# Reordering the steps ahead of the first feed-forward jobs in a gated mLSTM + spiking feed-forward kernel

## The reference

```
x1 = x  + tanh(g_xattn) * mlstm(layernorm(x), ctx, ctx)
out = x1 + tanh(g_ffn)  * ffn(layernorm(x1))

mlstm(q, k, v), per sequence, 8 heads of 32:
  ig, fg = [q,k,v] @ igate_w.T + igate_b, [q,k,v] @ fgate_w.T + fgate_b
  cs     = cumsum(log_sigmoid(fg))
  log_D  = cs[t] - cs[s] + ig[s]   (s <= t, else -inf);  m = rowmax(log_D)
  C      = (q k^T / sqrt(32)) * exp(log_D - m)
  h      = C / (max(|rowsum(C)|, exp(-m)) + 1e-6) @ v
  return layernorm(h) * ln_scale

ffn(x): y = square(relu(x @ W_fc.T)) @ W_proj.T      (256 -> 1024 -> 256)
        5 leaky integrate-and-fire steps on y; returns spikes / 5
```

## Time and profile before

| | before |
|---|---|
| median of 3 runs | 660.52 us (660.26 to 661.48) |
| span of the profiled execution | 661.2 us |
| TensorE matmul busy | 589.5 us, 89% |
| VectorE busy | 542.4 us, 82% |
| GpSimd busy | 485.6 us, 73% |
| ScalarE busy | 484.4 us, 73% |
| mean granted TensorE clock | 0.972 |

### The profile page before, as it was taken

How to read it: one execution, slowest core, us unless ns; L and a number is a source line. 1 busy time by engine, 2 the same in 40 slices (tenths; PEclk the granted TensorE clock), 3 DMA queues, 4 the chain that set the end, 5 groups by cost and what they waited for, 6 DMA issues and landing times.

```text
span 661.2 us, 17665 instructions
## 1 busy us (share of the span) xinstructions
PE 589.5 (89%) x6032; PEld 483.9 (73%) x6032; DVE 542.4 (82%) x1222; ACT 484.4 (73%) x1011; POOL 485.6 (73%) x531
## 2 busy tenths in 40 slices
...
GB/s 262 225 52 115 97 115 70 176 83 96 83 156 169 74 91 147 208 26 139 115 186 60 96 110 155 159 86 80 150 207 18 97 101 148 63 2 33 1 33 32
DMA packets 73192, 71.33 MB, mean 108 GB/s; under 512 B 8720, under 2 KB 68752, under 8 KB 73104
## 3 DMA queue, kind: packets, MB, share of 16 engines
...
## 4 chain that ended last, share of the span: by engine, by line
PE 51%; DVE 10%; issue 10%; ACT 7%; POOL 7%; SPq 4%; DMA 2%; POOLq 0%; ACTq 0%; DVEq 0%
PE z_ps L997 16%; PE y_ps L1057 16%; PE arg_ps L702 3%; PE qk_ps L717 3%; POOL sq_lo L1040 3%; DVE spikes L1075 3%; PE misc_ps L463 2%; SPq L650 2%; PE misc_ps L529 2%; SPq L513 2%; ACT sq_hi L1019 1%; POOL c_lo L746 1%; PE pv_ps L766 1%; PE pv_ps L764 1%; PE pv_ps L841 1%
## 5 line engine op out<-in xcount | busy, mean ns | idle before, releaser
L1040 POOL TENSOR_TENSOR sq_lo<-w_raw,sq_hi 128x512 fp32r<-128x512 f32 (+1 forms) x96 | 113.0, 1178 | 66.2 <-ACT w_raw L1020 66.1
L746 POOL TENSOR_TENSOR c_lo<-decay 128x512 bf16<-128x512 f32 x128 | 132.5, 1042 | 22.4 <-DVE decay L736 22.2
L997 PE MATMUL z_ps<-x_hi,wfc_hi 128*128 128x512 f32 (+1 forms) x288 | 115.7, 402 | 5.9 <-ACT w_raw L1007 4.1
L1057 PE MATMUL y_ps<-sq_hi,wpr_hi 128*128 128x512 f32 (+1 forms) x288 | 115.1, 400 | 1.1 <-POOL sq_lo L1040 1.1
L997 PE MATMUL z_ps<-x_hi,wfc_lo 128*128 128x512 f32 (+1 forms) x288 | 107.2, 372 | 0.0
L997 PE MATMUL z_ps<-x_lo,wfc_hi 128*128 128x512 f32 (+1 forms) x288 | 107.2, 372 | 0.0
L1057 PE MATMUL y_ps<-sq_lo,wpr_hi 128*128 128x512 f32 (+1 forms) x288 | 106.8, 371 | 0.0
L1057 PE MATMUL y_ps<-sq_hi,wpr_lo 128*128 128x512 f32 (+1 forms) x288 | 106.6, 370 | 0.0
L736 DVE TENSOR_TENSOR decay<-qk_ps,decay 128x512 f32<-128x512 f32 x128 | 87.1, 680 | 18.5 <-PE qk_ps L717 14.4
L728 ACT ACTIVATE decay<-arg_ps,lqk_col 128x512 f32<-128x512 f32 x128 | 86.5, 676 | 19.7 <-PE arg_ps L705 19.1
L1040 POOL TENSOR_TENSOR sq_lo<-relu,sq_hi 128x512 fp32r<-128x512 f32 (+1 forms) x48 | 56.3, 1173 | 37.9 <-ACT relu L1020 35.2
...
## 6 DMA issues: line engine op xcount, KB each, us to landing
...
```

What stands on the lines that cost most here:

```text
L746: e.tensor_tensor(c_lo[i % NCH][:, :], c, top(c), ALU.subtract).then_inc(sem("c_lo"), 1)
L997: ins = e.matmul(z_ps[:, tokens(q)], lhsT, rhs, start=(n == 0), stop=(n == len(terms) - 1))
L1040: e.tensor_tensor(sq_lo[n % NSQ][:, tokens(q)], relu[n % NRE][:, tokens(q)], sq_hi[n % NSQ][:, tokens(q)].bitcast(fp32), ALU.subtract).the ...
L1057: ins = e.matmul(y[:, c, :], w[:, j, c * P:(c + 1) * P], h, start=(j == 0 and i == 0 and (c == 0 or whole)), stop=(j == FT - 1 and i == 2) ...
```

## The change

The first steps of all five lists are put into another order; the lists hold the same steps as before. The loop over `SLOTS` becomes a loop over 1 to 5, its borders are moved by one to three steps (the last steps of the head become the first of the loop body), and what its last passes did is written out behind it in the same order; `MISC_ORDER` is written in another way and gives the same order. From these entries on the order is the old one: SyncE `load_m_rows(4)`, ScalarE `relu_step(1, 2)`, VectorE `cmul(3, 3)`, TensorE `z_step(1, 3)`, GpSimd `state_lo(3)`. The diff of the heads, in the order SyncE, ScalarE, VectorE, TensorE, GpSimd:

```diff
         def sync_program(e):
   load_x(e, 0)
+  load_x(e, 1)
+  load_values(e, 0)
+  load_x(e, 2)
   load_k(e, 0)
-  load_x(e, 1)
-  load_x(e, 2)
   load_x(e, 3)
-  load_values(e, 0)
+  load_x(e, 4)
+  load_x(e, 5)
   load_values(e, 1)
   load_k(e, 1)
+  load_k(e, 2)
+  load_x(e, 6)
   setup_load_wfc(e)
-  load_k(e, 2)
-  load_x(e, 4)
-  load_x(e, 5)
+  load_k(e, 3)
   stack_heads(e, 0)
-  stack_heads(e, 1)
-  load_k(e, 3)
   setup_load_wproj(e)
   load_a_rows(e, 0)
-  load_x(e, 6)
+  stack_heads(e, 1)
   load_k(e, 4)
+  load_values(e, 2)
   load_k(e, 5)
-  load_values(e, 2)
   load_a_rows(e, 1)
+  stack_heads(e, 2)
+  load_m_rows(e, 2)
+  load_x(e, 7)
   load_values(e, 3)
-  stack_heads(e, 2)
+  load_a_rows(e, 2)
   load_k(e, 6)
-  load_m_rows(e, 2)
+  load_a_rows(e, 3)
+  load_values(e, 4)
   load_k(e, 7)
-  load_x(e, 7)
-  load_a_rows(e, 2)
+  load_m_rows(e, 3)
   stack_heads(e, 3)
-  load_a_rows(e, 3)
-  load_m_rows(e, 3)
+  load_k(e, 8)
   load_x(e, 8)
-  load_values(e, 4)
   stack_heads(e, 4)
   load_x(e, 9)
   load_values(e, 5)
-  load_k(e, 8)
   load_m_rows(e, 4)
   load_a_rows(e, 4)
   load_m_rows(e, 5)
...
   setup_tanh(e)
   ln1_rstd(e, 0)
   ln1_apply(e, 0)
+  ln1_apply(e, 1)
   q_hi(e, 0)
-  ln1_apply(e, 1)
   q_hi(e, 1)
   gates_out(e, 0)
   gates_out(e, 1)
-  split_wfc_hi(e, 0)
+  ln1_rstd(e, 1)
   gate_softplus(e, 0)
-  ln1_rstd(e, 1)
   am_split(e, 0, 0)
   ln1_apply(e, 2)
   am_split(e, 0, 2)
+  split_wpr_hi(e, 0)
   gate_softplus(e, 1)
+  load_m_rows(e, 0)
   ln1_rstd(e, 2)
+  floor_exp(e, 0)
+  split_wfc_hi(e, 0)
   ln1_apply(e, 3)
-  load_m_rows(e, 0)
-  floor_exp(e, 0)
   q_hi(e, 2)
   am_split(e, 1, 0)
+  ln1_apply(e, 4)
   floor_exp(e, 1)
-  am_split(e, 1, 2)
   q_hi(e, 3)
   decay_exp(e, 0, 0)
-  ln1_apply(e, 4)
   decay_exp(e, 0, 1)
+  am_split(e, 1, 2)
+  gates_out(e, 2)
   decay_exp(e, 0, 2)
-  gates_out(e, 2)
+  split_wpr_hi(e, 1)
   q_hi(e, 4)
-  split_wpr_hi(e, 0)
-  split_wfc_hi(e, 1)
   load_m_rows(e, 1)
+  gates_out(e, 3)
   decay_exp(e, 0, 3)
-  gates_out(e, 3)
   gate_softplus(e, 2)
   decay_exp(e, 1, 0)
+  ln1_apply(e, 5)
   decay_exp(e, 1, 1)
   gates_out(e, 4)
+  decay_exp(e, 1, 2)
   am_split(e, 2, 0)
-  ln1_apply(e, 5)
+  floor_exp(e, 2)
+  split_wfc_hi(e, 1)
   am_split(e, 2, 2)
-  floor_exp(e, 2)
+  q_hi(e, 5)
   ln2_rstd(e, 0)
-  q_hi(e, 5)
-  split_wpr_hi(e, 1)
-  decay_exp(e, 1, 2)
+  ln3_rstd(e, 0)
   decay_exp(e, 1, 3)
-  ln3_rstd(e, 0)
+  gates_out(e, 5)
   ln3_apply(e, 0)
-  gates_out(e, 5)
   x2_hi_step(e, 0)
   ln1_rstd(e, 3)
   decay_exp(e, 2, 0)
   ln1_apply(e, 6)
+  decay_exp(e, 2, 1)
   relu_step(e, 0, 0)
-  decay_exp(e, 2, 1)
-  q_hi(e, 6)
-  ln1_apply(e, 7)
+  square(e, 0, 0)
   decay_exp(e, 2, 2)
   relu_step(e, 0, 1)
-  square(e, 0, 0)
+  ln1_apply(e, 7)
   ln2_rstd(e, 1)
+  square(e, 0, 1)
   relu_step(e, 0, 2)
-  square(e, 0, 1)
+  decay_exp(e, 2, 3)
+  q_hi(e, 6)
+  decay_exp(e, 3, 0)
   relu_step(e, 0, 3)
+  square(e, 0, 2)
   ln3_rstd(e, 1)
-  decay_exp(e, 2, 3)
-  square(e, 0, 2)
+  q_hi(e, 7)
   relu_step(e, 0, 4)
   square(e, 0, 3)
-  q_hi(e, 7)
   ln3_apply(e, 1)
-  decay_exp(e, 3, 0)
   square(e, 0, 4)
   x2_hi_step(e, 1)
+  decay_exp(e, 3, 1)
   relu_step(e, 0, 5)
-  square(e, 0, 5)
   ln2_rstd(e, 2)
-  relu_step(e, 0, 6)
   gates_out(e, 6)
   gates_out(e, 7)
-  decay_exp(e, 3, 1)
+  square(e, 0, 5)
+  relu_step(e, 0, 6)
   gate_softplus(e, 3)
+  relu_step(e, 0, 7)
   decay_exp(e, 3, 2)
-  relu_step(e, 0, 7)
+  am_split(e, 3, 0)
   square(e, 0, 6)
+  relu_step(e, 1, 0)
+  am_split(e, 3, 2)
   square(e, 0, 7)
-  am_split(e, 3, 0)
-  ln1_rstd(e, 4)
-  relu_step(e, 1, 0)
-  ln3_rstd(e, 2)
-  am_split(e, 3, 2)
   relu_step(e, 1, 1)
   floor_exp(e, 3)
+  ln3_rstd(e, 2)
   square(e, 1, 0)
   square(e, 1, 1)
+  ln1_rstd(e, 4)
   relu_step(e, 1, 2)
   decay_exp(e, 3, 3)
   ln3_apply(e, 2)
...
         def vector_program(e):
-  setup_rows(e, 1)
-  setup_cols(e)
   ln1_stats(e, 0)
   ln1_stats(e, 1)
+  setup_cols(e)
   ln1_offset(e, 0)
+  setup_rows(e, 1)
+  ln1_stats(e, 2)
+  ln1_stats(e, 3)
+  q_lo(e, 0)
   setup_gates(e)
-  ln1_stats(e, 2)
-  q_lo(e, 0)
   q_lo(e, 1)
-  ln1_stats(e, 3)
   setup_rows(e, 0)
   gate_pre(e, 0)
+  ln1_offset(e, 1)
   gate_cumsum(e, 0)
-  ln1_offset(e, 1)
   gate_cummax(e, 0)
   ln1_stats(e, 4)
+  ln1_stats(e, 5)
   am_split(e, 0, 1)
-  ln1_stats(e, 5)
+  ln1_stats(e, 6)
   am_split(e, 0, 3)
-  split_wfc_lo(e, 0)
   gate_pre(e, 1)
   setup_own(e)
   gate_cumsum(e, 1)
+  ln1_offset(e, 2)
   gate_cummax(e, 1)
   q_lo(e, 2)
+  q_lo(e, 3)
   am_split(e, 1, 1)
-  ln1_offset(e, 2)
-  q_lo(e, 3)
   cmul(e, 0, 0)
+  split_wpr_lo(e, 0)
+  am_split(e, 1, 3)
+  state_own(e, 0)
   cmul(e, 0, 1)
-  am_split(e, 1, 3)
+  q_lo(e, 4)
   cmul(e, 0, 2)
-  state_own(e, 0)
-  ln1_stats(e, 6)
-  q_lo(e, 4)
-  split_wpr_lo(e, 0)
-  split_wfc_lo(e, 1)
+  split_wfc_lo(e, 0)
   cmul(e, 0, 3)
   gate_pre(e, 2)
   gate_cumsum(e, 2)
...
   h_norm(e, 0)
   ln2_stats(e, 0)
   cmul(e, 1, 1)
+  q_lo(e, 5)
   x1_step(e, 0)
   cmul(e, 1, 2)
+  ln3_stats(e, 0)
+  split_wfc_lo(e, 1)
   state_own(e, 1)
-  ln3_stats(e, 0)
-  q_lo(e, 5)
   ln3_offset(e, 0)
   cmul(e, 1, 3)
+  split_wpr_lo(e, 1)
   ln1_stats(e, 7)
-  split_wpr_lo(e, 1)
   x2_lo_step(e, 0)
   ln1_offset(e, 3)
   cmul(e, 2, 0)
   h_norm(e, 1)
+  ln2_stats(e, 1)
   cmul(e, 2, 1)
-  ln2_stats(e, 1)
+  x1_step(e, 1)
+  cmul(e, 2, 2)
   q_lo(e, 6)
-  cmul(e, 2, 2)
-  x1_step(e, 1)
-  ln3_stats(e, 1)
   state_own(e, 2)
   cmul(e, 2, 3)
+  ln3_stats(e, 1)
   ln3_offset(e, 1)
-  ln1_stats(e, 8)
   q_lo(e, 7)
   h_norm(e, 2)
+  cmul(e, 3, 0)
   x2_lo_step(e, 1)
   ln2_stats(e, 2)
-  cmul(e, 3, 0)
   x1_step(e, 2)
   cmul(e, 3, 1)
+  ln1_stats(e, 8)
   gate_pre(e, 3)
   gate_cumsum(e, 3)
   gate_cummax(e, 3)
+  cmul(e, 3, 2)
   ln1_stats(e, 9)
   ln3_stats(e, 2)
   ln3_offset(e, 2)
-  state_own(e, 3)
-  cmul(e, 3, 2)
   ln1_offset(e, 4)
   spikes_step(e, 0, 0)
   spikes_step(e, 0, 1)
+  state_own(e, 3)
   cmul(e, 3, 3)
   spikes_step(e, 0, 2)
   spikes_step(e, 0, 3)
...
   gate_T(e, 1)
   floor_T(e, 0)
   q_T(e, 2)
-  qk(e, 0, 0)
   floor_T(e, 1)
   arg(e, 0, 0)
   q_T(e, 3)
+  qk(e, 0, 0)
   arg(e, 0, 1)
-  qk(e, 0, 1)
   gate_products(e, 2)
   arg(e, 0, 2)
+  q_T(e, 4)
+  arg(e, 0, 3)
   state(e, 0)
-  q_T(e, 4)
+  qk(e, 0, 1)
   qk(e, 0, 2)
-  arg(e, 0, 3)
   gate_products(e, 3)
+  pv(e, 0, 0)
+  qk(e, 0, 3)
   gate_T(e, 2)
-  qk(e, 0, 3)
-  pv(e, 0, 0)
   inter(e, 0)
   arg(e, 1, 0)
   qk(e, 1, 0)
+  arg(e, 1, 1)
   gate_products(e, 4)
-  arg(e, 1, 1)
   qk(e, 1, 1)
   pv(e, 0, 1)
+  arg(e, 1, 2)
   floor_T(e, 2)
   q_T(e, 5)
-  arg(e, 1, 2)
+  arg(e, 1, 3)
   qk(e, 1, 2)
+  qk(e, 1, 3)
   state(e, 1)
+  gate_products(e, 5)
   pv(e, 1, 0)
-  arg(e, 1, 3)
-  qk(e, 1, 3)
-  gate_products(e, 5)
+  qk(e, 2, 0)
   x2_T(e, 0)
+  pv(e, 1, 1)
   arg(e, 2, 0)
   inter(e, 1)
   arg(e, 2, 1)
-  qk(e, 2, 0)
-  pv(e, 1, 1)
   z_step(e, 0, 0)
   q_T(e, 6)
   arg(e, 2, 2)
-  qk(e, 2, 1)
   z_step(e, 0, 1)
   arg(e, 2, 3)
+  qk(e, 2, 1)
+  z_step(e, 0, 2)
   qk(e, 2, 2)
-  z_step(e, 0, 2)
+  y_step(e, 0, 0)
   z_step(e, 0, 3)
-  y_step(e, 0, 0)
+  arg(e, 3, 0)
   state(e, 2)
-  z_step(e, 0, 4)
   qk(e, 2, 3)
   q_T(e, 7)
-  arg(e, 3, 0)
   pv(e, 2, 0)
   inter(e, 2)
-  qk(e, 3, 0)
+  arg(e, 3, 1)
+  z_step(e, 0, 4)
   pv(e, 2, 1)
   y_step(e, 0, 1)
   z_step(e, 0, 5)
+  y_step(e, 0, 2)
   x2_T(e, 1)
-  y_step(e, 0, 2)
+  qk(e, 3, 0)
+  y_step(e, 0, 3)
+  qk(e, 3, 1)
+  gate_products(e, 6)
+  gate_products(e, 7)
   z_step(e, 0, 6)
-  gate_products(e, 6)
-  arg(e, 3, 1)
-  qk(e, 3, 1)
-  gate_products(e, 7)
   gate_T(e, 3)
-  y_step(e, 0, 3)
-  z_step(e, 0, 7)
+  qk(e, 3, 2)
   y_step(e, 0, 4)
   arg(e, 3, 2)
+  z_step(e, 0, 7)
   z_step(e, 1, 0)
   state(e, 3)
+  y_step(e, 0, 5)
   floor_T(e, 3)
-  y_step(e, 0, 5)
   z_step(e, 1, 1)
+  arg(e, 3, 3)
   y_step(e, 0, 6)
-  arg(e, 3, 3)
-  qk(e, 3, 2)
-  qk(e, 3, 3)
   y_step(e, 0, 7)
   z_step(e, 1, 2)
+  qk(e, 3, 3)
   z_step(e, 1, 3)
   pv(e, 3, 0)
   x2_T(e, 2)
...
         def gpsimd_program(e):
   setup_fixed(e)
+  setup_pool(e)
   k_hi(e, 0)
-  setup_pool(e)
-  v_hi_step(e, 0)
   k_lo(e, 0)
   k_hi(e, 1)
+  k_lo(e, 1)
+  v_hi_step(e, 0)
   v_hi_step(e, 1)
-  k_lo(e, 1)
+  k_hi(e, 2)
   v_lo_step(e, 0)
+  k_lo(e, 2)
   v_lo_step(e, 1)
-  k_hi(e, 2)
-  k_hi(e, 3)
-  k_lo(e, 2)
   k_weigh(e, 0)
   k_weigh_lo(e, 0)
+  k_hi(e, 3)
   c_lo_step(e, 0, 0)
   k_lo(e, 3)
-  k_hi(e, 4)
   c_lo_step(e, 0, 1)
   k_weigh(e, 1)
+  c_lo_step(e, 0, 2)
   state_lo(e, 0)
-  c_lo_step(e, 0, 2)
+  k_hi(e, 4)
+  c_lo_step(e, 0, 3)
   k_lo(e, 4)
-  c_lo_step(e, 0, 3)
-  k_hi(e, 5)
   k_weigh_lo(e, 1)
   am_split(e, 2, 1)
+  c_lo_step(e, 1, 0)
   am_split(e, 2, 3)
-  c_lo_step(e, 1, 0)
+  k_hi(e, 5)
+  c_lo_step(e, 1, 1)
+  v_hi_step(e, 2)
   k_lo(e, 5)
-  c_lo_step(e, 1, 1)
   c_lo_step(e, 1, 2)
+  c_lo_step(e, 1, 3)
+  v_lo_step(e, 2)
+  k_weigh(e, 2)
   state_lo(e, 1)
   k_hi(e, 6)
+  square_lo(e, 0, 0)
+  c_lo_step(e, 2, 0)
   k_lo(e, 6)
-  k_weigh(e, 2)
-  c_lo_step(e, 1, 3)
-  v_hi_step(e, 2)
```

(98 more changed lines are left out.)

590 lines of the change are left out of this document (571 added, 19 removed), and 3 rows, old and new, of the table order.

## The result

| | before | after |
|---|---|---|
| median | 660.62 us (659.87 to 663.08, 7 runs) | 667.12 us (662.97 to 670.0, 7 runs) |
| ratio | | 1.0094, 95% interval 1.0066 to 1.0123 |
| span of the profiled execution | 661.2 us | 665.3 us |

The kernel after is slower, by 0.7 to 1.2%, some 6 us. The forecast was 659.9 us, and 667.12 is above the whole range.

What follows compares the result with a forecast made beforehand. SyncE's unbroken queue from 100.60 us, begun by am_split(3,3), was taken to fix TensorE's full stretch; leads of 1.9, 0.3, 2.0, 2.0, 1.2 ended at 0.6: span 661.2 - 0.6 = 660.6, median 0.7 lower, 659.9 us (657.2 to 662.3).

Steps and rivals of the forecast that it cites:

- The frame: SyncE's unbroken queue from 100.60 us, begun by am_split(3,3), sets qk(5,0), TensorE's full stretch and the end; 0.6 us earlier.
- rival D: At SyncE's queue start, 100.60 us: another chain meets it, so nothing changes, 660.5 us; chance 0.44 together with the forecast.
- Checkpoint 2: Down to q_T(3): ScalarE and VectorE steps now in front nearly use up the lead; 36.35 against 36.69 us, lead 0.3.
- A (faster): Losses between first z step and am_split(3,3) fall into idle time; lead 2.0 to 2.8 us lives, 658.1 us; chance 0.36.
- C (late stack): SyncE's stack_heads(3), issued 3.5 us later, delays k_hi(7) past 2 us of cover; 661.9 us at 4; chance 0.07 with the like.
- B (clock): TensorE's clock rises later than about 76 us; each z or y step at low level costs 0.75; 662.2 us; chance 0.13.
- 1: second q_T: Loads at the start: x1 issued earlier lands 1.2 us sooner, q_lo(1) gains 1.9; lead (old start minus new) 1.9 us.
- 3: last write of the scan: Down to the scan of group 2: gate_products(2) and gate_pre(2) wait less; 54.85 to 52.9 us, lead 2.0.
- 4: z_step(0,0): Down to the first z step: 68.6 against 71.43 us, lead 2.8 with bare durations, 2.0 after contention.
- 5: x2_T(1): Down to x2_T(1): ln1_apply(7) moved in front, TensorE without a wait from q_T(7) to qk(3,0); 84.8 against 86.00, lead 1.2.
- 6: am_split(3,3): Down to the end of group 3's gate chain: cmul(3,0), z_step(0,6), ln1_stats(8) stand in front; lead 0.6 us.
- port contention: On the path to the first z step: moved splits wfc_lo(0), wfc_lo(1) lose up to 1.0 us each beside GpSimd; 0.8 taken.

Runs made afterwards that it cites:

- step moved back: Kernel after with ScalarE's split_wpr_hi(0) moved from behind am_split(0,2) to behind floor_exp(1); 661.61 us, ratio to before 0.9999.
- The step alone in the kernel before: Kernel before with only ScalarE's split_wpr_hi(0) moved forward behind am_split(0,2); 665.53 us, ratio to before 1.0059.
- the wait made longer: Kernel after with SyncE's w_proj load moved behind load_a_rows(0), issued at 29.68 us; 670.56 us, ratio to before 1.0126.
- the front trim: Kernel after with split_wpr_hi(0) behind floor_exp(1), and ln1_stats(6), ln1_stats(8), k_hi(8) out of am_split(3,3)'s way; 661.42 us, ratio to before 0.9993.
- both edits: Kernel after: split_wpr_hi(0) behind floor_exp(1), steps before am_split(3,3) thinned out, stack_heads(5) ahead of load_m_rows(5) on SyncE; 661.87 us, ratio to before 0.9993.
- stack first: Kernel after with split_wpr_hi(0) behind floor_exp(1), and SyncE's stack_heads(5) ahead of load_m_rows(5), load_k(9), load_a_rows(5); 662.48 us, ratio to before 0.9998.
- stack first in before: Kernel before with only SyncE's stack_heads(5) ahead of load_m_rows(5), load_k(9), load_a_rows(5); also the second execution of the old order; 662.71 us, ratio 1.0014.

## Why the prediction was wrong

**The frame, that the end moves as the start of SyncE's stretch does, held roughly for delays.** SyncE's stretch moved by 4.2 us, qk(5,0) by 4.75 and h_norm(3) from 121.17 to 126.83, 5.7. Of the first step 0.5 is the landing of the last transfer (4.99 against 4.47 us); it was 4.97 with the step moved back too. The next 0.9 goes with a granted clock of 0.89 on TensorE, where 1.00 stands before: qk(5,0) and the transposes behind it take 0.61 and 0.85 us in the chain instead of 0.40 and 0.44.

```profile
116.00:132.00 16.00, 11.14 (x152) 10.30 (x151) 12.26 (x35) 9.87 (x25) 12.13 (x16) 0.89 0.80 131
```

By count_T(0) it is 6.7, and the median rose by 6.5. The step alone in the kernel before gave 3.45 at SyncE and 3.5 in time. But with the wait made longer 4.8 more at SyncE gave 2 to 3.4 more time, so that a delay passes in full is not shown.

For leads the change itself is no test of it, because its lead of 0.6 cannot be told from the spread between two executions. SyncE's stretch with the step moved back begins at 100.00: 0.6 before the profiled execution of before, but 0.2 behind the second one (99.76). The ratio of 0.9999 fits that. Where there was a lead, in the front trim, part of it was gone at h_norm(3) and all of it behind the loads of x. That is close to rival D: another chain, over TensorE, VectorE and ScalarE, is there at almost the same time.

**Checkpoint 2 is the step that failed.** It lists what ScalarE does between am_split(0,2) and q_T(3): softplus(1), the issue of m_rows(0) and so on. split_wpr_hi(0), first in that list in the diff, is not in it. Missing are its 1.06 us, of which 0.3 count, and its wait, 4.55 us. The other split in that stretch, split_wfc_hi(0), is in the list, rightly and without a wait. The lead of 0.3 at q_T(3) became a loss of 4.6. Two things had to be seen: that the step is there, and that it is the first reader of a load, which the kernel before has in place only near 31.3 us, where the new order reaches the step at about 26.6. The new order issues the load earlier (20.51 instead of 24.79), so the 5 to 6 us of before must not be added to that either: the load of w_fc, issued at 5.72 before, now goes out at 12.25, and k3 (256 KB), eight stack transfers of 128 KB and the two halves of w_proj (512 KB each) stand behind its 1024 KB. That is 3.4 MB; at the 216 GB/s that the kernel before moves from 18 to 28 us it takes some 16 us, which puts the end near 28 us, an estimate. It was 31.1. Either number says that the step waits.

**None of the rivals had it either.** A (faster) and C (late stack) were not seen. Stack(3) was issued from 72.42 to 77.57 us with the step moved back, inside to slightly behind my 70 to 75; k_hi(7) ran at 82.24 without a wait, and in the run with both edits with one of 0.3 us. C's cover holds, with no margin instead of 2 us. B (clock) is no cause, though its sign is there: the granted clock of the kernel after is 0.50 until 78 us. The two executions of the old order part there too: the profiled one has half the clock from 56 to 72 us and the other the full clock, and yet the distance between them hardly grows, from 0.77 us at z_step(0,0) (71.43, 70.66) to 0.83 at am_split(3,3) (99.38, 98.55). In the new order the runs "step moved back" and "stack first" have the same steps up to here, and one had the full clock where the other had half of it:

```profile
60.00:68.00 8.00, 4.99 (x91) 4.27 (x92) 7.64 (x17) 3.34 (x9) 7.30 (x6) 1.00 0.37 105
68.00:76.00 8.00, 6.91 (x60) 6.31 (x57) 5.08 (x15) 6.20 (x12) 4.37 (x7) 1.00 0.45 124
```

```profile
60.00:68.00 8.00, 5.12 (x92) 4.38 (x93) 7.64 (x17) 3.35 (x9) 7.30 (x6) 0.50 0.37 105
68.00:76.00 8.00, 7.08 (x54) 6.54 (x52) 4.96 (x15) 5.96 (x11) 4.37 (x7) 0.62 0.46 126
```

Their z_step(0,0) starts at 70.65 and 70.53 and their am_split(3,3) at 98.79 and 99.09: half the clock in the head goes with some 0.4 us, not with the 0.75 per step of rival B.

**The other checkpoints** can be judged in the run with the step moved back, against both executions of the old order (start in us; forecast with its lead, measured with its lead over the first and the second):

| | before | stack first in before | forecast | step moved back |
|---|---|---|---|---|
| 1: second q_T | 14.32 | 13.59 | (1.9 at q_lo(1)) | 12.68 (1.6; 0.9) |
| 2: q_T(3) | 36.69 | 35.94 | 36.35 (0.3) | 36.77 (-0.1; -0.8) |
| 3: last write of the scan | 54.85 | 54.09 | 52.9 (2.0) | 54.15 (0.7; -0.1) |
| 4: z_step(0,0) | 71.43 | 70.66 | 69.4 (2.0) | 70.65 (0.8; 0.0) |
| 5: x2_T(1) | 86.00 | 85.19 | 84.8 (1.2) | 84.92 (1.1; 0.3) |
| 6: am_split(3,3) | 99.38 | 98.55 | 98.8 (0.6) | 98.79 (0.6; -0.2) |

Against the rows that the prediction had, the loads (1) and the end (5, 6) look as worked out. Against the second execution half of the lead from the loads is the late landing of x1, the prediction's "5.9 us later", and nothing is left at the end. So a second term was mis-sized: the 1.2 us put on x1's earlier load is 1.1 over the profiled execution (reader at 6.59 against 7.68), but 0.35 over the second one (6.95). In 3 the mechanism was right up to the scan's start: gate_pre(2) began 1.9 earlier (48.67 against 50.55; 1.1 by the second). The scan and the operation behind it then took 1.2 longer, and that is the port contention, put on the wrong instructions: of the two that the prediction looked at, wfc_lo(0) took 1.40 us instead of 1.21, and the c_lo beside it 2.02 instead of 1.03. VectorE and GpSimd with the step moved back:

```profile
49.62 1.40 DVE L603 TENSOR_TENSOR_SCAN cs<-am_rest 16x256 f32<-16x256 f32 x1
51.06 1.20 DVE L604 TENSOR_TENSOR am<-i_pre,cs 16x256 f32<-16x256 f32 x1
...
49.45 1.03 POOL L748 TENSOR_TENSOR c_lo<-decay 128x512 bf16<-128x512 f32 x1
50.45 1.54 POOL L436 TENSOR_TENSOR kT_lo<-kT_in,kT_hi 128x512 bf16<-128x512 f32 x1
```

The scan took 0.79 and the operation behind it 0.65 before. In the stack-first run, same instructions, the scan happened to start 0.11 us ahead of c_lo, and the other one paid:

```profile
49.34 0.68 DVE L603 TENSOR_TENSOR_SCAN cs<-am_rest 16x256 f32<-16x256 f32 x1
...
49.45 1.40 POOL L748 TENSOR_TENSOR c_lo<-decay 128x512 bf16<-128x512 f32 x1
```

This is what the Trainium skill states (SBUF — State Buffer, "Who interferes with whom"): VectorE, when an instruction has two inputs in SBUF, and GpSimd, when it reads SBUF, contend for a shared pair of ports under an exclusive lock, and the second waits. These rows agree, and show that a scan is subject to it too. Over the profiled execution of before, the lead was 0.8 at z_step(0,0) and not 2.0, and still 1.1 at x2_T(1): the loss of 0.8 that checkpoint 5 forecast did not come, though TensorE had work without a wait from q_T(7) to qk(3,0), as it says. That the end shows the forecast 0.6 is luck twice over: 1.2 too much lead and 0.8 too much loss nearly cancel, and the lead that is left is the late x1 of one execution.

**Span and median.** I took the median as the span less 0.7. In every run the time is the span of that same execution plus 1.8 (667.12 with 665.3; 661.55 with 659.8), so the profiled execution of before was one of 663.0, 2.4 over the median: a late one. Hence spans differ by 4.1 and medians by 6.5. Single executions of one kernel differ by 6 to 8 us (659.8 to 666.25 with the step moved back, 658.88 to 666.99 in the kernel before); these differences lie behind 140 us as well. In the profiled execution of the step moved back, 3.1 us of TensorE's busy time are missing between 212 and 284 us against the same stretch before (68.49 against 71.64), and 4.1 of VectorE's (61.32 against 65.38).
